# The one-hot of the chosen path: transposed once and spread by one 16-row product per tile of paths, in place of eight products from broadcast columns

## What is computed

```python
x = x + attention(layernorm(x), ctx, ctx, mask, Wq, bq, Wk, bk, Wv, bv, Wo, bo)
...
x_mixed = mix(layernorm(x))                      # three-point mix along the sequence
h = einsum('bsd,pdm->bspm', x_mixed, W1) + b1    # 9 paths of 64 values
stacked_paths = einsum('bspm,pmd->bspd', h, W2) + b2
scores = tanh(x_mixed @ Wo1 + bo1) @ Wo2 + bo2
idx = argmax(scores, axis=-1)
weights = one_hot(idx, 9)
collapsed = einsum('bspd,bsp->bsd', stacked_paths, weights)
x = x + layernorm(x + collapsed, gamma, beta)
```

## Time and profile before

| | us |
|---|---|
| median of three runs | 342.62 |
| lowest and highest of them | 341.48, 344.41 |
| the profiled execution, whole | 342.44 |
| its span | 340.6 |
| PE busy | 304.6 (89%) |
| DVE busy | 272.8 (80%) |
| POOL busy | 201.1 (59%) |
| ACT busy | 179.7 (53%) |

### The profile page before, as it was taken

The page is one execution under the profiler, slowest core; times in us unless marked ns, Lnnn a source line. Parts: engine busy times, 40 slices in busy tenths (PEclk is TensorE's granted clock), DMA queues, the critical chain, the costliest instruction groups (busy, mean ns, idle before and its releaser), DMA issues.

```text
span 340.6 us, 7016 instructions
## 1 busy us (share of the span) xinstructions
PE 304.6 (89%) x2700; PEld 224.8 (66%) x2700; DVE 272.8 (80%) x623; ACT 179.7 (53%) x279; POOL 201.1 (59%) x240
## 2 busy tenths in 40 slices
PE   1698789689999999999999999999999998989980
PEld 1574364456579766886769577876778577857970
DVE  2775898998489797989798897988597857685796
ACT  1454824725942777267652776177444853548320
POOL 0254002672495299727883599719881878139975
PEclk9979999999999999999999999999999999999997
DMA  8941200010020010200120010000100010001003
GB/s 222 235 119 41 77 2 3 0 57 23 3 78 0 2 62 2 79 1 1 64 79 2 0 64 2 0 2 1 64 2 1 3 64 0 0 2 62 3 0 123
DMA packets 20570, 13.14 MB, mean 39 GB/s; under 512 B 10097, under 2 KB 20410, under 8 KB 20538
## 3 DMA queue, kind: packets, MB, share of 16 engines
q1 hardware_dynamic: 18898, 12.14, 12.2%
q10 hardware_dynamic: 1640, 0.57, 0.8%
HBM read 8.51 MB, written 4.19 MB: 37 GB/s over the span
## 4 chain that ended last, share of the span: by engine, by line
PE 66%; DVE 19%; ACT 6%; issue 4%; POOL 3%; DMA 1%; DVEq 0%; SPq 0%; POOLq 0%; ACTq 0%
PE ps L444 13%; PE ps L610 6%; PE ps L449 6%; PE ps L697 4%; PE ps L592 4%; PE ps L567 4%; PE ps L698 4%; PE ps L702 4%; PE ps L586 4%; PE ps L677 3%; DVE mx L1181 2%; PE ps L503 2%; DVE st L1127 2%; DVE osb L1208 2%; PE ps L570 2%
## 5 line engine op out<-in xcount | busy, mean ns | idle before, releaser
L1481 POOL TENSOR_TENSOR rs<-ve,halfneg 128x4 f32<-128x4 f32 x22 | 25.1, 1141 | 83.8 <-DVE ve L1144 83.8
L885 ACT ACTIVATE e<-ps 128x1024 f32<-128x1024 f32 x32 | 31.1, 1023 | 16.4 <-PE ps L574 16.4
L1181 DVE TENSOR_REDUCE mx<-ps 128x16 f32<-128x1024 f32 x32 | 38.0, 1217 | 0.3 <-PE ps L542 0.3
L1562 POOL TENSOR_TENSOR hml<-hs,hmh 128x512 fp32r<-128x512 f32 x28 | 35.0, 1276 | 5.3 <-ACT hmh L946 5.3
L697 PE MATMUL ps<-w2h,hmh 128*128 128x256 f32 (+1 forms) x140 | 35.6, 289 | 0.0
L698 PE MATMUL ps<-w2l,hmh 128*128 128x256 f32 (+1 forms) x140 | 34.7, 282 | 0.0
L936 ACT ACTIVATE hs<-ps,b1s 128x512 f32<-128x512 f32 x28 | 19.3, 691 | 23.4 <-PE ps L449 23.2
L610 PE MATMUL ps<-wo,osb 128*128 128x256 f32 x128 | 31.4, 390 | 0.0
L1301 DVE TENSOR_TENSOR hs<-hs,ps 128x512 f32<-128x512 f32 x28 | 18.6, 684 | 15.6 <-PE ps L677 15.6
L910 ACT ACTIVATE xh<-x,vb,rs 128x256 f32<-128x256 f32 x24 | 12.5, 593 | 33.0 <-POOL vb L1494 33.0
L1527 POOL TENSOR_TENSOR y<-xh2f,gms 128x256 f32<-128x256 f32 x24 | 20.4, 880 | 16.0 <-DVE xh2f L1153 16.0
(11 more groups left out here) (166 smaller groups left out, 784.0 us busy)
## 6 DMA issues: line engine op xcount, KB each, us to landing
xin<-in_x SPq DMA_DIRECT2D x8, 512.0 KB, 3.7
out<-y SPq DMA_DIRECT2D x7, 512.0 KB, 2.8
min_<-in_mask_Bx1xSxS_ik SPq DMA_DIRECT2D x8, 128.0 KB, 4.6
hs<-in_L_ffn_W SPq DMA_DIRECT2D x2, 288.0 KB
hs<-in_L_ffn_W SPq DMA_DIRECT2D x1, 512.0 KB
out<-xin SPq DMA_DIRECT2D x2, 256.0 KB, 2.6
cst<-in_constants SPq DMA_DIRECT2D x1, 384.0 KB, 6.4
e<-in_ctx ACTq DMA_DIRECT2D x1, 256.0 KB, 4.4
```

The source lines that it names most:

```text
L885: nc.scalar.activation(e[:, 2 * i:2 * i + 2, :], ps[:, bank:bank + 2, :], ACT.Exp).then_inc(s_e, 1)
L1181: v.tensor_reduce(mx[:, k, :].rearrange("p (a h) -> p a h", a=2), ps[:, bank:bank + 2, :].rearrange("p a (h s) -> p a h s", s=SK), AX.X, A ...
L1481: g.tensor_tensor(ln[7][:, :], ln[6][:, :], halfneg[:, :], ALU.pow).then_inc(s_r, 1)
L1562: g.tensor_tensor(L.lo(m, r), L.selected(m, r), L.hi(m, r).bitcast(F32), ALU.subtract).then_inc(L.s_hl, 1)
```

## The change

The one-hot gets 16 columns instead of 64. `onehot_transposed` turns it by four products (16 columns of weights, the identity as moving operand) into 16 rows x 512 tokens in a PSUM bank, ACT's `onehot_copy` copies those rows to the new buffer `ohT` in bf16, and `rep` is one product a tile: 16 rows of a constant matrix as weights (`paths`: row p is one in the 64 columns of path p; for the last tile also the 9 columns of the diagonal), `ohT` as moving operand, 512 columns. The constants are loaded by one more transfer on SP. In a step the four transposes stand between the P V products and the denominators; they wait for `oh` (s_oh). The transposed one-hot takes the bank of the gate's scores, so the next use of that bank, h2, waits for ACT's copy instead of DVE's `gidx`, and `gidx` gets a semaphore of its own. Behind the steps the transposes of the chunk (3,0) use bank 3 and those of (3,1) bank 5, and one `w1` tile of (3,1) moves ahead of rep0 of (3,0).

```diff
@@ layer_program @@
-        oh = sb("oh", [P, NT, DM], BF16)
+        oh = sb("oh", [P, NT, PR], BF16)
+        ohT = sb("ohT", [PR, CH], BF16)
+        paths = sb("paths", [PR, NM * P // 2])
+        path_rows = paths[:, :].bitcast(BF16)
@@ sync @@
+            load(paths[:, :], consts[0:PR, C_R:], s_pr)
@@ tensor: pv @@
                 mm.then_inc(s_o, 1)
+                if f:
+                    onehot_transposed(*f)
 
                 for p in range(NPAIR):
@@ tensor: take_slot @@
-                        if act:
+                        if act == "gate":
+                            pe.wait_ge(L.s_gate, at(b, NJ, reads))
+                        elif act == "act":
                             pe.wait_ge(L.s_fa, at(b, NJ * NFA, reads))
@@ tensor @@
+            def onehot_transposed(b, j, L=usual):
+                pe.wait_ge(s_oh, at(b, NJ, j + 1))
+                for k in range(NT):
+                    mm = nc.tensor.transpose(bf16_bank(L.onehot_bank(j))[0:PR, k * P:(k + 1) * P], oh[:, k, :], ident_b)
+                mm.then_inc(s_ohp, 1)
+
             def rep(b, j, m, L=usual):
 
                 o = take_slot(b, j, f"rep{m}", L)
                 if m == 0:
-                    pe.wait_ge(s_oh, at(b, NJ, j + 1))
-                for k in range(NT):
-                    ks = slice(k * P, (k + 1) * P)
-                    for a in range(2):
-                        p = 2 * m + a
-                        if p < NPATH:
-                            sel = oh[:, k, p:p + 1].broadcast_to([P, DM])
-                            mm = nc.tensor.matmul(o[a * DM:(a + 1) * DM, ks], sel, ident_b, start=True, stop=True)
-                        else:
-                            mm = nc.tensor.matmul(o[DM:, ks], oh[:, k, :], ident_b,
-                                                  start=True, stop=True)
-                mm.then_inc(L.s_f, 1)
+                    pe.wait_ge(s_ohc, at(b, NJ, j + 1))
+                r = rows_of(m)
+                nc.tensor.matmul(o[0:r, :], path_rows[:, m * P:m * P + r], ohT[:, :], start=True, stop=True).then_inc(L.s_f, 1)
@@ scalar @@
+            def onehot_copy(b, j, L=usual):
+                act.wait_ge(s_ohp, at(b, NJ, j + 1))
+                nc.scalar.activation(ohT[:, :], bf16_bank(L.onehot_bank(j))[0:PR, :], ACT.Copy).then_inc(s_ohc, 1)
@@ scalar: layernorm1_apply(b, j, f) @@
                 for k in range(NT // 2 if (b, j) == (0, 0) else NT):
+                    if f and k == NT // 2:
+                        onehot_copy(*f)
@@ scalar: step @@
                 if after and f:
-                    layernorm1_apply(*after)
+                    layernorm1_apply(*after, f)
+                elif f:
+                    onehot_copy(*f)
```

More of the change, by code:

```diff
@@ L34 @@
 P = 128
+PR = 16
 B, S, D = 4, 1024, 256
@@ L60 @@
 C_BC = C_CST
-C_N = C_BC + KD * P
+C_R = C_BC + KD * P
+C_N = C_R + NM * P // 2
 def as_bf16(ones, word=0x3F80):
@@ L93, in constants @@
     c[:, C_IO:C_IO + NPATH] = np.arange(NPATH) - NPATH
+    col = np.arange(NM * P)[None, :]
+    path = np.where(col < 4 * P + DM, col // DM, col - 4 * P - DM)
+    c[:, C_R:C_R + NM * P // 2] = as_bf16((r == path) & (r < NPATH))
     return c
@@ L305, in count, with reader, onehot_bank @@
                 return at(b, NJ * per, j * per + n)
+            def reader(self, use):
+                return {"h": "act", "g": "gate"}.get(use[0], "dve")
+            def onehot_bank(self, j):
+                return self.bank(j, "gate")
             def bank(self, j, use):
@@ L325, in layer_program, with onehot_bank @@
         class BehindSteps(Usual):
+            def onehot_bank(self, j):
+                return 3
             uses = ["h0", "h4", "h1", "gate", "h2", "h3", "rep0", "rep1", "rep2", "rep3", "rep4", "w2a", "w2b"]
-            by_act = [u in ("h4", "h0", "h1", "h2", "h3") for u in uses]
         class Last(Path):
@@ L340, in count, with onehot_bank @@
                 return n
+            def onehot_bank(self, j):
+                return 5
             def bank(self, j, use):
@@ L361, in layer_program @@
         behind = BehindSteps(s_f, s_fa, s_fv, s_hh, s_hl)
+        usual.s_gate, behind.s_gate = s_ohc, s_gidx
         last_y = xin[:, 1]
@@ L630, in take_slot @@
                     elif use == "w2a":
+                        pe.wait_ge(s_ohc, B * NJ)
+                    elif use == "w2b":
                         pe.wait_ge(L.s_fv, 1)
-                    elif use == "w2b":
+                    elif use == "w2c":
                         pe.wait_ge(L.s_fv, 2)
-                    elif use == "w2c":
-                        pe.wait_ge(L.s_fv, 3)
                 else:
@@ L641, in take_slot @@
                     else:
-                        act = L.by_act[before % NU]
-                        reads = sum(L.by_act[i % NU] == act for i in range(before + 1))
-                        if act:
+                        readers = [L.reader(use) for use in NJ * L.uses][:before + 1]
+                        act, reads = readers[-1], readers.count(readers[-1])
+                        if act == "gate":
+                            pe.wait_ge(L.s_gate, at(b, NJ, reads))
+                        elif act == "act":
                             pe.wait_ge(L.s_fa, at(b, NJ * NFA, reads))
@@ L810, in _ @@
             w1(*f0, 3, behind)
+            onehot_transposed(*f0, behind)
+            w1(*f1, 4, last)
             rep(*f0, 0, behind)
             rep(*f0, 1, behind)
-            w1(*f1, 4, last)
+            w1(*f1, 0, last)
             rep(*f0, 2, behind)
-            w1(*f1, 0, last)
+            w1(*f1, 1, last)
             rep(*f0, 3, behind)
-            w1(*f1, 1, last)
             rep(*f0, 4, behind)
@@ L821, in _ @@
             w1(*f1, 3, last)
+            onehot_transposed(*f1, last)
             for m in range(NM):
@@ L1026, in _ @@
             hidden(*f0, 3, behind)
+            onehot_copy(*f0, behind)
             keep_xh2(*f0)
@@ L1037, in _ @@
             hidden(*f1, 3, last)
+            onehot_copy(*f1, last)
             for m in range(NM):
@@ L1316, in residual_row_stats @@
             def residual_row_stats(b, j, group, L=usual):
-                dve.wait_ge(L.s_fv, L.read_by_dve(b, j, NFV - 1 + group))
+                dve.wait_ge(L.s_fv, L.read_by_dve(b, j, NM + 1 + group))
                 row_stats(L.x, TAIL_LN[L is last], L.w2[group]).then_inc(s_ln3s, 1)
```

17 lines of the change are left out of this document (9 added, 8 removed).

## The result

The changed kernel takes 347.16 us, the median of four runs (345.15 to 347.88); the kernel before took 342.77 (341.48 to 344.41, four runs beside them). The ratio is 1.012, with a 95% interval of 1.0088 to 1.0152: the changed kernel is slower by 1.2%, which is more than its interval and less than 2%. The forecast was 345.7 us, with a range of 343.2 to 347.2. The profiled execution of after took 347.74 us, its span 345.9; that of before 342.44 and 340.6.

A forecast was written before the change was run, and what follows sets the result against it. PE was taken to bound the six steps, with a DVE stretch ahead of the spread. Wait 2.46, transposes 1.38 and reps -0.54 summed to +3.3 us on 342.44: 345.7 us, range 343.2 to 347.2.

The forecast's parts named there:

- The wait: Ahead of the denominators, PE waits for DVE's one-hot, mostly in steps 2 to 4: 2.46 us in sum.
- the 0.4 that was named as a sign: PE's timeline should show 0.4 to 0.9 us idle ahead of the transposes in steps 2 to 4.
- The transposes: Four products ahead of the denominators on PE's path, 0.23 us in each of six steps: 1.38 us.
- The reps: One 16-row product at 0.31 us instead of eight at 0.34; 18 reps on PE's path: -0.54 us.
- ACT's copy: Copying the transposed one-hot out of PSUM takes 0.60 us, with 2.5 us of cover before the spread: cost 0.
- Banks and the small transfer: h2's wait for the copy and the extra load at the start: cost 0, or one issue's time.
- POOL's order is not touched: In the steps, POOL keeps its order and gets the low parts' inputs later by what PE is late.
- Rival D: Shifted DVE work shares less with POOL, so waits in steps 2 to 4 mostly go: 343.5 to 344.5 us; chance 0.10.
- Behind the steps: POOL bounds the last two chunks; PE's hole of about 1 us costs 0, bounds -0.3 and +0.5.
- the forecast's own sign (over 0.5 us): The forecast is wrong if the part behind step 6 is longer or shorter by over 0.5 us.
- B: 16-row reps don't change the array's shape; 18 reps give 2.3 to 4.1 us: 342.2 to 344.0 us; chance 0.20.
- C: ACT's copy or semaphores cost 2.5 us more than thought, so the spread waits for osb: 347.2 us; chance 0.12.

The follow-up runs named there:

- e2_wait: The kernel before with only PE's wait for the one-hot ahead of the denominators added; 344.94 us, ratio 1.0055.
- e3_wait_transposes: The kernel before with PE's wait for the one-hot and four transposes whose result nobody reads; 346.61 us, ratio 1.0113.
- e4_old_reps: The changed kernel with every rep made of the eight old products again, transposes and ACT's copy kept; 347.0 us, ratio 1.0122.
- e10_mid_pool_waits: The changed kernel with the transposes in the middle of the denominators and one group of POOL's additions held until rDs is written; 344.83 us, ratio 1.0072.
- before_again: The kernel before, unchanged, run and traced a second time; 343.29 us, ratio 1.0035.
- after_again: The changed kernel, unchanged, run and traced a second time; 348.0 us, ratio 1.0165.
- after_third: The changed kernel, unchanged, run and traced a third time; 347.22 us, ratio 1.0149.
- e9_pool_waits: The changed kernel with POOL holding one group of additions in each step until DVE has written rDs; 347.16 us, ratio 1.0131.

## Why the forecast was right, and where it was off

The main mechanism and the direction are as forecast; the time is 1.5 us above the value given and 0.04 us inside the upper end of the range. There is luck in that: the medians of the two later groups of the changed kernel, 347.22 and 348.0, lie outside it, and the largest chance, 0.54, was on a change too small to be told, under about 1%, where 1.2% was measured. By its own steps:

1. *The wait*, 2.46 us: e2_wait shows 2.56, of which about 0.3 is the slow cast of its step 3, so 2.3. In after the waits of steps 2 to 4 are 0.83, 0.40 and 0.83 us where 0.90, 0.45 and 0.89 were taken; their brackets say 0.65, 0.22 and 0.65, and the 0.22 is under the 0.4 that was named as a sign. The start follows the one-hot by 0.06 us, less than the 0.1 taken. Right, in place and size.
2. *The transposes*, 1.38 us: in step 4 of after they add 0.21, near the 0.23 taken. Over six steps e3_wait_transposes adds 1.86 to e2_wait, of which the casts' share is about 0.9 in steps 1, 5 and 6 (what these add above 0.2), while step 3's faster cast hides 0.2. At 0.2 a step the transposes are about 1.2. Too dear by 0.2.
3. *The reps*, -0.54 us: e4_old_reps gives -0.2. The row was well chosen (208.37 to the next product at 208.68 is 0.31), but less of it reaches the spread: in steps 2 to 4 of after PE waits 0.16 us for rDs ahead of it. Mis-sized by 0.3, in the other direction. Terms 2 and 3 together, +0.84, are tested by e10_mid_pool_waits, in which PE waits neither for the one-hot nor, in steps 1, 5 and 6, for rDs: +0.78. Its steps 1, 2, 4, 5 and 6 are 0.10 to 0.20 longer than before; step 3 is not (-0.02), and there DVE's cast and product are faster than before (0.23 and 0.35 us for 0.38 and 0.91). Without that help it would be about +1.0, which is 1.2 - 0.2.
4. *ACT's copy*: the copy took 0.59 us, and that of the P V products was over 2.7 us before the spread. Cost 0 holds.
5. *Banks and the small transfer*: the spread ahead of step 1 starts at 66.03 against 65.90, and before_again has 66.09: cost 0 holds.
6. *POOL's order is not touched*: true, and here the step failed. It asked who waits for POOL, and not what POOL runs beside. Rival D did name that DVE's products run slower beside POOL's, but only as a gain, and set it aside because both "keep their distance". They don't: in step 1 DVE moved by 0.34 us and POOL by 0.09, and the cast of rDs came to lie beside an addition: PE waits 0.43 us more in steps 1 and 5, and another 0.38 in step 6 in the profiled trace. This is the missing term, 0.4 us; what step 6 lost came back in the tail.
7. *Behind the steps*: PE's hole is 1.02 us where "about 1 us" was forecast. By after_again the tail is 52.20 against 52.11 us: cost 0.1, inside the bounds, where the clock is full. In the traces of after and after_third it is 1.15 and 1.6 us longer, with the low clock in the rows above, and by the forecast's own sign (over 0.5 us) this step was wrong there: it had no term for the clock behind the hole.

The sum made anew from the runs is 2.3 + 1.2 - 0.2 + 0.4 = +3.7 us for the steps without the slow cast in step 6; the traces have +3.7 to +4.2, the forecast +3.3. The tail adds 0.1 at full clock. The median is 4.4 us above that of before in the first comparison, 5.7 beside after_again (348.0 and 342.32) and 4.65 beside after_third (347.22 and 342.57). Up to 1.7 us of this is in no step. All three traces of after have stretches at half clock that cost 1.5 to 1.6 us, and neither trace of before has one that costs anything; e2_wait and e9_pool_waits have none that costs either. The times say the same: of the 15 executions of after 11 lie more than 1.5 us above the fastest (345.15), of the 52 of before beside the experiments only 11 (fastest 341.59), of the 12 of e2_wait none. So the changed kernel seems to meet costly stretches more often. For those in the tail the hole is the suspect, by the count above. For those among the first chunks the change can't be: e3_wait_transposes runs the kernel before's own instructions up to step 1, and its spread ahead of step 1 starts at 67.57 us. How often each comes, and so how it shares out over the medians, stays open. The fastest executions of the first comparison lie 3.67 us apart (345.15 and 341.48), which is what the steps alone give.

Of the rivals, B (the reps lose their shape's cost) is refuted by the row of 0.31 us and by e4_old_reps; C (ACT) by the 2.7 us; D (the one-hot comes earlier) by the waits of 0.83, 0.40 and 0.83. By the Trainium skill (TensorE: Matmul & The Clock Gate, Back-to-back issue gap) a rep would have taken 0.216 us; the measurement, 0.31, decides against it for a product that stands alone among other shapes. The five reps in a row in the tail, 1.24 us with the last one's own 0.38, are 0.215 us apart, close to that figure; the other 0.1 us is lost beside neighbours of another shape. The middle steps came out at 38.3, 37.9 and 38.3 us where 38.2, 37.8 and 38.2 were forecast.

No version that I ran beats the kernel before. The nearest, e10_mid_pool_waits, has +0.8 us in its steps, and that is the price of the transposes less what the reps give back; with reps at 0.31 us instead of 0.34 that exchange can't pay.

## What to carry to other kernels

When a product is moved ahead of others on the busiest engine, price the moment at which its operand is ready before the product itself: here 2.3 of 3.7 us were a wait that did not exist two us later in the same order, and putting the transposes half a group later took it away. Fewer instructions of the same length in columns are hardly a gain: eight narrow products side by side took 0.34 us and one product 0.31. And ask of each engine that shifts what it will then run beside, not only who waits for it. Where a change opens idle time on TensorE, look at the granted clock behind it in more than one trace.

## What the runs showed of the hardware

DVE's cast of 128x128 elements from f32 to fp32r takes 0.23 us with POOL at rest and 0.57 to 0.88 us where it runs beside POOL's additions; the scalar_tensor_tensor behind it takes 0.35 and 0.73. With a wait of POOL on DVE both go back in the steps in which it holds the additions (e9_pool_waits).

A bf16 product of 16 rows and 512 columns costs 0.31 us between products of other shapes and 0.215 us behind its like.

The granted clock falls to 1.2 GHz for 3 to 7 us ahead of PE's last product in 12 of the 14 kept traces, and the place differs from run to run of the same kernel (at 321 us in after and after_third, at 34 and 45 us in after_again, at 22 us in the first trace of before, nowhere ahead of the last product in before_again). Where PE is on the path a kernel's stretches cost 1.5 to 2.4 us in one part of it (66.1 against 68.48 in the column "ahead", 85.2 against 86.8 in step 6 and tail), as much as half of the change under study.
